# An audio tower in one program block, with an expert's places as 64 slots by 16 blocks

## The reference

```
d  = first differences of x over time;  e = d @ W_ve + b_ve              (16, 750, 128)
h  = (ewma(e) + reversed ewma(e)) / 2 @ W_lin + b_lin                    # forward and backward smoothing
n  = layernorm(h);  q, k, v, g = n @ wq, wk, wv, wg  (+ biases)          # 8 heads of 16
h  = h + silu(g) * ((q k / 4 * gamma_h**(i - j), j <= i) v)              # decaying linear attention
m  = layernorm(h) as 12000 rows;  p = softmax over all rows of m @ Wr    # 8 experts
per expert e: the 1024 rows with the largest p[:, e];
   out[row] += p[row, e] * (gelu(m[row] @ W1[e] + b1[e]) @ W2[e] + b2[e])
result: h + out
```

## Time and profile before

| | |
|---|---|
| median of 3 runs | 631.08 us (630.94 to 636.57) |
| profiled execution, its own time | 635.75 us |
| its span, first to last instruction | 634.0 us |
| mean granted clock of PE | 0.851 of full speed |
| busy: PE, PEld, DVE, ACT, POOL | 488.3, 350.0, 406.6, 288.4, 355.2 us |

### The profile page before, as it was taken

The page is one execution under the profiler, slowest core; times in us unless marked ns, Lnnn a source line. Parts: engine busy times, 40 slices in busy tenths (PEclk is TensorE's granted clock), DMA queues, the critical chain, the costliest instruction groups (busy, mean ns, idle before and its releaser), DMA issues. The chain is left out here.

```text
span 634.0 us, 15489 instructions
## 1 busy us (share of the span) xinstructions
PE 488.3 (77%) x6262; PEld 350.0 (55%) x6262; DVE 406.6 (64%) x797; ACT 288.4 (45%) x545; POOL 355.2 (56%) x267
## 2 busy tenths in 40 slices
PE   4799989999899999999724543258779797797880
PEld 3457656776477777777514442235555565556650
DVE  5444895768766677777647777875766767765110
ACT  1455643556435666666204442036444563445640
POOL 7047743577335865555400000176787878888874
PEclk9889997999889999999955555559797897987996
DMA  6210132132222323321241000012442534424232
GB/s 242 56 33 4 44 83 66 37 84 58 67 77 56 84 51 79 79 78 54 56 122 38 0 0 1 7 35 57 64 78 50 70 63 62 76 48 72 49 30 25
DMA packets 45139, 37.01 MB, mean 58 GB/s; under 512 B 5842, under 2 KB 39186, under 8 KB 44948
## 3 DMA queue, kind: packets, MB, share of 16 engines
q1 hardware_dynamic: 33176, 25.85, 15.1%
q0 software_dynamic: 11264, 8.72, 10.2%
q10 hardware_dynamic: 636, 1.54, 0.7%
HBM read 12.89 MB, written 16.96 MB: 47 GB/s over the span
## 5 line engine op out<-in xcount | busy, mean ns | idle before, releaser
L752 POOL TENSOR_TENSOR prob<-prob,cst 125x1000 f32<-125x1000 f32 x48 | 102.6, 2138 | 87.6 <-ACT prob L639 87.6
L1393 POOL DMA_INDIRECT out<-y,idx_add x64 | 101.8, 1590 | 18.3 <-issue 16.9
L639 ACT COPY prob<-ps_score 125x1000 f32<-125x1000 f32 x48 | 47.6, 992 | 90.5 <-PE ps_score L418 90.4
L1371 POOL DMA_INDIRECT taken<-rows_dram,idx x64 | 69.8, 1091 | 19.3 <-issue 18.7
L1543 DVE TENSOR_TENSOR slot_hot<-numbers,bank 125x4096 bf16<-125x4096 bf16 x18 | 79.4, 4412 | 0.0
L1250 PE MATMUL bank<-takenT,w_sb 128*128 128x512 f32 x128 | 71.7, 700 | 1.7 <-ACT hidden L1325 1.1
L1259 PEld LDWEIGHTS bank<-w_sb,hidden 128*128 128x128 f32 x512 | 58.4, 192 | 24.1 <-ACT hidden L1325 24.1
L1259 PE MATMUL bank<-w_sb,hidden 128*128 128x128 f32 x512 | 61.3, 278 | 11.7 <-ACT hidden L1325 11.7
L1325 ACT ACTIVATE hidden<-bank,b_sb 128x512 f32<-128x512 f32 x64 | 43.6, 687 | 51.7 <-PE bank L1250 51.6
L886 DVE TENSOR_TENSOR prob<-ps_score,cst 125x1000 f32<-125x1000 f32 x48 | 57.4, 1196 | 9.1 <-PE ps_score L418 9.0
L1360 POOL TENSOR_TENSOR carrier<-cst 1x1 f32<-1x1 f32 x25 | 10.1, 403 | 94.6 <-DVE idx L1556 88.7
(11 more groups left out here) (184 smaller groups left out, 919.7 us busy)
## 6 DMA issues: line engine op xcount, KB each, us to landing
rows_dram<-row_sb SPq DMA_DIRECT2D x16, 404.3 KB
out<-row_sb SPq DMA_DIRECT2D x16, 375.0 KB
w_sb<-in_L_ffn_W SPq DMA_DIRECT2D x16, 256.0 KB
r_in<-smooth SPq DMA_DIRECT2D x32, 93.8 KB, 3.7
e_in<-s_norm SPq DMA_DIRECT2D x32, 93.8 KB, 2.1
cst<-in_consts SPq DMA_DIRECT2D x1, 1703.0 KB
xin<-in_x ACTq DMA_DIRECT2D x4, 375.0 KB, 7.3
taken<-rows_dram,idx POOLq DMA_INDIRECT x64, 2.6
```

The costliest lines, as they stand in the source:

```text
L639: act.copy(prob[no % 2][:, 2:4, :, :].rearrange("p g c i -> p g (c i)"), ps_score[0:C, 2:4, 0:4 * C]).then_inc(high_copied, 1)
L752: pool.tensor_tensor(scores, scores, const("mask", C)[:, H // 2 * C:].rearrange("p (g i) -> p g i", g=2) .unsqueeze(2).broadcast_to([C, 2, ...
L1371: pool.indirect_dma_start(out=taken[it.slot][:, g, :], out_offset=None, in_=rows_dram[:, :], in_offset=bass.IndirectOffsetOnAxis(ap=idx[it ...
L1393: pool.indirect_dma_start(out=out_rows[:, :], out_offset=bass.IndirectOffsetOnAxis(ap=idx_add[it.slot][:, g:g + 1], axis=0), in_=y[it.slot ...
```

## The change

It does six things. (1) The two blocks become one; PE and SP wait for the last copy of the logits instead of a block's end. (2) The value products have 128 columns; ACT writes each head's 16 columns into a buffer `v_split` with zeros between, which DVE sets once at the start; POOL's masked weights go. (3) A third row buffer. (4) In a smoothing step the sum and the row statistics move into the next step, behind the states and the first low scores. (5) PE gets products that nobody reads: seven at the end of the first stage, and `keep_warm` ones in the search, behind it and in the first lists. (6) Places split into 64 slots (6 bits) and 16 blocks; the 16 blocks stand as 8 even and 8 odd ones, each tile takes two matmuls with weights of 125 by 64, the even ones into PSUM partitions 0 to 63 and the odd ones into 64 to 127, so that the sum has the same layout as before. `SLOTS` is 64, `ROW_BUFS` 3 and `SPLIT` 2 * D + 2 * DH; the buffers' shapes follow. The diff, cut to its core and moved twelve columns to the left:

```diff
@@ -425,9 +424,9 @@
     o = claim(f"a{p}", it)
-    pe.wait_ge(read[f"v{p}"], it + 1)
-    if p == 2:
-        pe.wait_ge(read["v3"], it + 1)
+    pe.wait_ge(read["v0" if p else "v1"], it + 1)
+    if no == 0:
+        pe.wait_ge(zeros_set, 2)
     if p == 0:
@@ -502,33 +501,19 @@
-def token_units(it):
-    ps = [claim(f"t{k}", it) for k in range(2)]
+def token_units(it, name, w):
+    ps = [claim(f"{name}{k}", it) for k in range(2)]
     for c in range(HALF):
...
                           e_in[it % PER_BLOCK][at:at + CH + 2, chunk(k * HALF + c)],
-                          w_raw[at:at + CH + 2, 1, :], start=True, stop=True)
+                          w_raw[at:at + CH + 2, w, :], start=True, stop=True)
             if c == HALF - 1:
-                m.then_inc(filled[f"t{k}"], 1)
-
-def value_units(it, ks):
...
+                m.then_inc(filled[f"{name}{k}"], 1)
...
     pe.wait_ge(read["t1"], it + 1)
-    pe.wait_ge(read["v2"], it + 1)
+    pe.wait_ge(read["v0"], it + 1)
     ps = claim("s", it)
@@ -591,14 +576,16 @@
     if after is not None:
-        token_units(after)
+        token_units(after, "t", 1)
         scores(after, 0)
-        value_units(after, (0, 1))
-        value_units(after, (2, 3))
+        token_units(after, "v", 2)
     if own is not None:
...
 all_steps(step)
+pe.wait_ge(high_copied, B * PAIRS)
+for k in range(7):
+    pe.matmul(ps_score[:, 3, :], const("centre"), const("projections"), start=True, stop=True)
@@ -655,12 +642,12 @@
 def rows(it, k):
-    if k == 0 and it >= 2:
-        act.wait_ge(logits_kept, it - 1)
-        act.wait_ge(h2_out[it % 2], it // 2 * 16)
-        act.wait_ge(rows_out[it % 2], it // 2 * 16)
+    if k == 0 and it >= ROW_BUFS:
+        act.wait_ge(logits_kept, it - ROW_BUFS + 1)
+        act.wait_ge(h2_out[it % ROW_BUFS], it // ROW_BUFS * 16)
+        act.wait_ge(rows_out[it % ROW_BUFS], it // ROW_BUFS * 16)
     act.wait_ge(filled[f"o{k}"], it + 1)
...
@@ -673,12 +660,13 @@
 def values_out(it, k):
-    if k == 0 and it >= 2:
+    if k == 1 and it >= 2:
         act.wait_ge(valued, (it - 1) * PAIRS)
     act.wait_ge(filled[f"v{k}"], it + 1)
-    first, n = VALUE_CHUNKS[k][0], len(VALUE_CHUNKS[k])
-    act.copy(v_split[it % 2][:, first:first + n, :].rearrange("p c d -> p (c d)"),
-             bank_of(f"v{k}", it)[0:C, 0:n * 2 * D]).then_inc(read[f"v{k}"], 1)
+    own_half = v_split[it % 2][:, k * HALF:(k + 1) * HALF, :].rearrange("p c (e y) -> p c e y", e=2)
+    act.copy(own_half[:, :, :, 0:D].rearrange("p c e (g z) -> p c e g z", z=2 * DH)[:, :, :, :, 0:DH],
+             bank_of(f"v{k}", it)[0:C, 0:HALF * D].rearrange("p (c g e d) -> p c e g d", c=HALF, e=2, d=DH)
+             ).then_inc(read[f"v{k}"], 1)
...
@@ -718,7 +706,7 @@
         high_scores(after, 0)
-        for k in range(4):
+        for k in (1, 0):
             values_out(after, k)
...
@@ -804,6 +782,8 @@
 dve.memset(diff[:, 0:1], 0.0).then_inc(diff_done, 1)
+for k in range(2):
+    dve.memset(v_split[k][:, :, :], 0.0).then_inc(zeros_set, 1)
...
@@ -979,6 +959,10 @@
         low_scores(own, 1)
+    if n - 1 in SMOOTH_AT:
+        smooth_sum(SMOOTH_AT[n - 1])
+        norm_stats(last, 0)
+        norm_stats(last, 1)
     if last is not None:
@@ -1001,13 +985,11 @@
         smooth_backward(j)
-    if before is not None:
+    if before is not None and not j:
         norm_stats(before, 0)
...
         gated_out(own, 2)
-    if j:
-        smooth_sum(j)
     if n in POWER_AT:
...
@@ -1161,6 +1141,7 @@
+sp.wait_ge(logits_kept, B)
 load(item(0))
@@ -1170,11 +1151,18 @@
+def keep_warm(n, to, width=512):
+
+    for k in range(n):
+        pe.matmul(to[:, 0:width], const("centre"), const("projections")[:, 0:width], start=True, stop=True)
+
+pe.wait_ge(logits_kept, B)
 for c in range(NC):
...
+keep_warm(2, banks[7])
 pe.wait_ge(dve_step, 2)
@@ -1182,6 +1170,7 @@
           start=True, stop=True).then_inc(ends_spread, 1)
+keep_warm(1, banks[7])
 with pe.Fori(0, ROUNDS // UNROLL) as i:
@@ -1190,41 +1179,53 @@
+        keep_warm(5, banks[7], 128)
         pe.wait_ge(counted_act, r + 1)
...
                   skip_group_check=True).then_inc(totals_done, 1)
-
+        keep_warm(2, banks[7], 128)
+
+keep_warm(6, banks[7])
 pe.wait_ge(rows_ranked, 1)
...
           skip_group_check=True).then_inc(offsets_done, 1)
+keep_warm(3, banks[3])
 pe.wait_ge(place_done, 1)
...
+keep_warm(5, banks[3])
+
 def index(it):
...
         if t % (TILES // HOT_PARTS) == 0:
+            if early(it, 1) and t:
+                keep_warm(1, banks[3])
             pe.wait_ge(hot_done, it.no * HOT_PARTS + t // (TILES // HOT_PARTS) + 1)
-        m = pe.matmul(ps_idx[:, 0:2 * G], slot_hot[it.slot][:, t // RUN, :, t % RUN],
-                      block_val[it.slot][:, t // RUN, :, t % RUN],
-                      start=(t == 0), stop=(t == TILES - 1))
+        for odd in range(2):
+            vals = block_val[it.slot][:, t // RUN, odd, :, :].rearrange("p k (g r) -> p (k g) r", r=RUN)
+            m = pe.matmul(ps_idx[odd * SLOTS:(odd + 1) * SLOTS, 0:2 * G],
+                          slot_hot[it.slot][:, t // RUN, :, t % RUN], vals[:, :, t % RUN],
+                          start=(t == 0), stop=(t == TILES - 1), skip_group_check=True)
     m.then_inc(idx_ps, 1)
...
+keep_warm(4, banks[3])
 pe.wait_ge(exp_sums_done, 1)
 pe.matmul(banks[4][:, 0:E], const("ones"), exp_sums[:, :], start=True, stop=True).then_inc(sums_spread, 1)
+keep_warm(8, banks[3])
 pe.wait_ge(inverse_done, 1)
...
@@ -1497,18 +1498,18 @@
     dve.wait_ge(split_step, step + 2)
-    dve.tensor_scalar(block_int[:, mine, :], place_tok[:, mine, :], 7, None, ALU.arith_shift_right)
-    dve.tensor_scalar(slot_int[:, mine, :], place_tok[:, mine, :], 127, None,
+    dve.tensor_scalar(block_int[:, mine, :], place_tok[:, mine, :], 6, None, ALU.arith_shift_right)
+    dve.tensor_scalar(slot_int[:, mine, :], place_tok[:, mine, :], SLOTS - 1, None,
                       ALU.bitwise_and).then_inc(split_step, 1)
...
-at = 128 * RUN
+at = SLOTS * RUN
 slot_nos = numbers16[0:C, 0:at].rearrange("p (s t) -> p s t", t=RUN).unsqueeze(1)
-block_nos = numbers16[0:C, at:at + G * RUN].rearrange("p (s t) -> p s t", t=RUN).unsqueeze(1)
-at += G * RUN
+block_nos = numbers16[0:C, at:at + 2 * G * RUN].rearrange("p (s t) -> p s t", t=RUN).unsqueeze(1)
+at += 2 * G * RUN
 tile_nos = numbers16[0:C, at:at + TILES].rearrange("p (u t) -> p u t", t=RUN).unsqueeze(2)
@@ -1525,23 +1526,26 @@
             dve.tensor_copy(own, slot16[:, mine, :].rearrange("p a t -> p (a t)")).then_inc(slots_kept, 1)
-        dve.tensor_tensor(block_hot[:, :, :, :], block_nos.broadcast_to([C, RUNS, G, RUN]),
-                          blocks.broadcast_to([C, RUNS, G, RUN]), ALU.is_equal).then_inc(hot_step, 1)
+        hot_by_block = block_hot[:, :, :, :].rearrange("p u o (g r) -> p u (o g) r", r=RUN)
+        dve.tensor_tensor(hot_by_block, block_nos.broadcast_to([C, RUNS, 2 * G, RUN]),
+                          blocks.broadcast_to([C, RUNS, 2 * G, RUN]), ALU.is_equal).then_inc(hot_step, 1)
         if not early(it, 2):
...
         dve.wait_ge(hot_step, it.no + 1)
-        dve.tensor_scalar(block_val[it.slot][:, :, 0:G, :], block_hot[:, :, :, :], const("partition", C), None,
+        dve.tensor_scalar(block_val[it.slot][:, :, :, 0, :], block_hot[:, :, :, :], const("partition", C), None,
                           ALU.mult)
-        dve.tensor_tensor(block_val[it.slot][:, :, G:2 * G, :], block_hot[:, :, :, :],
-                          tile_nos.broadcast_to([C, RUNS, G, RUN]), ALU.mult)
+        for odd in range(2):
+            dve.tensor_tensor(block_val[it.slot][:, :, odd, 1, :].rearrange("p u (g r) -> p u g r", r=RUN),
+                              block_hot[:, :, odd, :].rearrange("p u (g r) -> p u g r", r=RUN),
+                              tile_nos.broadcast_to([C, RUNS, G, RUN]), ALU.mult)
     n = RUNS // HOT_PARTS
...
         runs = slice(k * n, (k + 1) * n)
-        dve.tensor_tensor(slot_hot[it.slot][:, runs, :, :], slot_nos.broadcast_to([C, n, 128, RUN]),
-                          slots[:, runs].broadcast_to([C, n, 128, RUN]), ALU.is_equal).then_inc(hot_done, 1)
+        dve.tensor_tensor(slot_hot[it.slot][:, runs, :, :], slot_nos.broadcast_to([C, n, SLOTS, RUN]),
+                          slots[:, runs].broadcast_to([C, n, SLOTS, RUN]), ALU.is_equal).then_inc(hot_done, 1)
```

More of the change, by code:

```diff
@@ L88, in unit_order @@
         if after:
-            order += [(u, n + 1) for u in ("t0", "t1", "v0", "v1", "v2", "v3")]
+            order += [(u, n + 1) for u in ("t0", "t1", "v0", "v1")]
         if own:
@@ L151, in constants @@
         "partition": p[:, None],
-        "even_odd": np.concatenate([np.broadcast_to(head % 2 == k, (128, 128)) for k in range(2)], axis=1),
         "half": np.full((128, NC * PER_BLOCK), -0.5),
         "numbers": np.broadcast_to(np.concatenate([
-            np.repeat(np.arange(128), RUN), np.repeat(np.arange(G), RUN),
```

(52 more changed lines are left out.)

35 lines of the change are left out of this document (13 added, 22 removed).

## The result

The changed kernel takes **611.42 us** (median of 3; 610.14 to 611.74) against 631.08: ratio 0.9656, 95% interval 0.9575 to 0.9738. Faster, inside the range of 578 to 615, but with half of the gain that I forecast. The profiled executions took 635.75 (span 634.0) and 610.14 (608.3).

| stretch | before | after | gain | forecast |
|---|---|---|---|---|
| to the end of PE's last product of the first block | 312.29 | 293.25 | 19.0 | 26 |
| to the router's transposes | 12.59 | 5.84 | 6.8 | 8 |
| to the first round | 7.13 | 6.17 | 1.0 | 1 |
| sixteen rounds | 52.40 | 50.47 | 1.9 | 6.4 |
| last round to the first gather | 24.09 | 26.42 | -2.3 | 0 |

A forecast was written before the change was run, and what follows sets the result against it. PE's order of work bounds the first stage, short DVE-ACT-PE steps the search, list chain and POOL nearly tied the loop. Terms sum to -42.4 from the profiled 635.75, giving 593.3; predicted 590, between 588.7 and 593.3, range 578 to 615.

The forecast's parts named there:

- Values: First stage, value product of 128 instead of 256 columns: state loads 0.8 earlier in 15 items, -12 us (-9.6 to -14).
- Smoothing: First stage, sum and statistics moved behind the next states: two items start states earlier and PE avoids half clock, -14 us.
- rival 4: First stage: the smoothing's stop only moves to the next item, DVE having the same work there; 601 us, chance 0.14.
- The other end that I gave, -17: Far bound of the smoothing gain for two items, against -2.8 if PE stops at the next item instead.
- End of the first block: Third row buffer frees ACT's last rows and PE waits for the logits alone: -8 us, -4 if rows still wait.
- Rounds: Threshold search, sixteen rounds: fill products raise the clock, 0.42 less a round with the hand-over kept, -6.4 us.
- Rival 3: Threshold search: fills hold the rounds, clock stays low, each round 1.7 longer; 623 us, chance 0.10, mostly near 610.
- First lists: Ahead of the loop: shorter slot lists against doubled block lists and slower PE thirds, 0 us, from -5 to +5.
- Loop: Experts' loop: list chain falls to 24.2 a period, below POOL's 25.68; -1 us over it, between -2.8 and +3.
- Rule against trace: Index products: the skill's loading rules give an estimated 53 ns for 64 columns, 10.2 us a list, about 621 us.
- rival 1: Index products: 64-column loads are dear and one after another, 0.06 each; 633 us, chance 0.10 for 600 to 633.
- three conditions for being wrong: Index products over 0.05 apart, rounds longer than 3.3, or PE stopping anew in the items behind the smoothing.

The follow-up runs named there:

- both masks: Changed kernel with POOL's mask product for each item's second pair, and in four steps the next item's first pair, waiting for DVE's state scan: 595.37 us, 0.9407.
- last run: Changed kernel with both mask products waiting for DVE's state scan, and the smoothing's sum and row statistics back at their old places: 606.57 us, 0.9575.
- lists 128 by 8: Changed kernel with the earlier kernel's lists, 128 slots by 8 blocks and 96 index products a list: 608.23 us, 0.9601.
- both half-add runs: Changed kernel without the output's indirect adds of odd 128-row groups: 603.61 us with 64 slots by 16 blocks, 597.26 (one run) with 128 by 8.

## Why the prediction was right, and where its sizes were off

**Values** ("I take 0.8 for 15 items: -12"). Right mechanism, too small: the last four items went from 15.70 on average to 14.70 from state to state, 1.0 each; for 15 items that is 15, an estimate from these four. The pace is the same with the smoothing put back and with two row buffers, so it comes from neither; I did not run the narrower products alone, so that they are the cause is argued from the timeline at an item's end.

**Smoothing** ("-14 for two") is the step that failed. The first stage gained 19.0; with 15 for the values some 4 are left. From state to state the four periods behind the smoothing (third state to fifth, seventh to ninth) got 12.5 shorter, 8.5 without the values, and the other eleven 6.2 instead of 11: part of the gain was lost again behind the row roots, for which my sum had no term. My rival 4 had the right form (the stop only moves), but put it on DVE's added work. The runs show another cause: **DVE's scans, its sum and its wide copy, which work from SBUF, stand still while POOL's mask product runs.** The scan ended 0.34 behind POOL's product (137.92 against 137.58), while the products between them, which read PSUM, took their usual 0.31; with one wait put ahead of POOL's product the same scan takes 0.49. The change brought DVE's state scan of four items into POOL's 2.14; two of the four are there with the smoothing put back too, so the move brought only the other two. The Trainium skill ("SBUF — State Buffer", Who interferes with whom) says that a DVE instruction with two SBUF inputs, or a copy in a two-port mode, and a GpSimd instruction that reads SBUF exclude each other, and that the second to issue waits for the first; the trace agrees. In the earlier trace rows I read the durations 3.72 and 2.70 as the cost of the work; alone the backward scan takes 1.77 and the sum 0.94. POOL's timeline of the kernel before, which I did not set beside them, has a mask product in each:

```profile
160.00 2.14 POOL L752 TENSOR_TENSOR prob<-prob,cst 125x1000 f32<-125x1000 f32 x1 [1.68 <-ACT prob L639]
...
164.88 2.13 POOL L752 TENSOR_TENSOR prob<-prob,cst 125x1000 f32<-125x1000 f32 x1 [2.74 <-ACT prob L639]
```

With both masks moved the whole stage gained 31.9, and the four periods behind the smoothing 19.9, 15.9 without the values: the -14 was there to be had. The move is worth 8.4 of the 31.9 (last run). The other end that I gave, -17, is too far by my own terms: two times 8.1 is 16.2.

**End of the first block** (-8): 6.8. The third buffer gives 2.6 of it; with two buffers 4.2 remain, which I put down to the joining of the blocks; that was not run alone. The seven fills, to which I gave no price, outlast the logits by 1.4; with five the gain is 8.05.

**Rounds** (-6.4): right at the full clock, 2.91 to 3.02 apart (0.4 less, as the sum has it; from 1.05 and 0.60 it would be 0.45, not the 0.42 that I wrote), but I took the clock for granted. PE is idle for a quarter of the 6 us ahead of the rounds; the granted clock falls to 0.50 (1.2 GHz), and three rounds at half clock, with twelve passes in front of the two matmuls on the path, take 4.35, 1.03 more than before (I had given 1.7). With the first-stage stops gone it was one round, with five fills none: 46.17, a gain of 6.2. Rival 3 happened in part.

**First lists** (0, from -5 to +5): +4.8, at the edge. One third of a list takes PE 2.09 where it took 1.23, and the path goes through PE, not through DVE's halved slot lists. The split costs 5.3 here (lists 128 by 8). The fills behind the rounds cost 3.8 in the kernel with both masks, but only 0.5 in the changed kernel itself (74.05 against 73.55 without any).

**Loop** (-1): 2.1, within the bound of 2.8. Index products at 0.0305, not 0.028. I expected PE to wait longer; instead PE became the chain. It is busy 24.26 of a period of 25.82, and the two waits of 0.78 for ACT make up the rest; before it was busy 20.75 of 25.68 (columns as in the earlier trace rows, the kernel after first). POOL adds 0.5 to it, no more.

```profile
481.59:507.41 25.82, 24.26 (x282) 17.38 (x280) 12.66 (x17) 12.94 (x22) 21.18 (x20) 0.85 0.39 66
...
559.14:584.82 25.68, 20.75 (x185) 14.86 (x183) 14.95 (x13) 11.80 (x20) 21.05 (x19) 0.84 0.39 66
```

**Rule against trace.** From 64 columns in a column tile the Trainium skill ("TensorE: Matmul & The Clock Gate", LDWEIGHTS and Weight-path perf modes) led me to an estimated 53 ns and 621 us; the products came 30.5 ns apart, so the measurement decides against that reading, and rival 1 with it.

Of my three conditions for being wrong two came true in part (three rounds over 3.3, PE stops anew). The total is inside the range because the range had room for rival 4 and a part of rival 3; the forecast of 590 itself was 21 too low.

## What to carry to other kernels

Before calling a long DVE duration work, set it beside POOL's timeline: where the same shape is short elsewhere and the long one's end follows the end of a POOL instruction, it holds a wait; two waits on POOL that let DVE's short instructions go first were worth 16 us here, nearly as much as the whole change. Fill products pay only while the engine they hold up is not next on the path, so they are to be counted out to the moment at which the next real product is ready. When a list is halved on one engine and doubled on another, look at which of them ends last at each place where it is used: the same split cost 5.3 ahead of the loop and gave 2.4 in it.

## What the runs showed of the hardware

The granted clock fell while PE was busy without a gap. Stretches of the kernel after in one period (columns as in the earlier trace rows): narrow products of 16 columns (471 to 476.9), then full-width ones at the half clock.

```profile
471.00:474.00 3.00, 3.00 (x101) 3.00 (x102) 2.97 (x3) 0.88 (x3) 2.45 (x4) 1.00 0.62 126
474.00:476.90 2.90, 2.90 (x99) 2.88 (x97) 0.27 (x1) 0.00 (x0) 2.60 (x2) 0.75 0.63 56
476.90:481.00 4.10, 4.10 (x10) 2.16 (x9) 3.80 (x8) 2.56 (x3) 3.49 (x4) 0.50 0.39 36
```

It costs (1.12 - 0.60) + (5.85 - 3.79) = 2.6 in this period, which no one of these kernels got back. In the first list it fell in the same way: 0.99 from 374.0 to 376.5 and 0.50 from 376.5 to 381.0, with PE busy throughout. The kernel before pays a like price behind its lists (its turn took 1.09 at 503.32, 0.60 at 496.23), but there PE had been idle for 3.30. And where in the first stage the clock falls differs between executions: six profiled ones with the same first-stage program (the changed kernel, no fills, both half-add runs, lists 128 by 8) or nearly the same (two row buffers) ended it between 289.86 and 295.68, of which up to 1.8 lie ahead of the first state. With both masks it ended at 278.60, 280.26 and 280.36, and once, in the longest of five executions, at 288.86. What decides that was not settled.
